# A six-layer decoder kernel: each VectorE filter, convolution and norm instruction waits for its own predecessor instead of for the last one issued

## The reference, cut to what matters

```python
x = _layernorm(x + L0_attn(x));  x = _layernorm(x + L0_xattn(x, ctx));  x = _layernorm(x + L0_ffn(x))   # a, b, c
x = _layernorm(x + L1_attn(x));  x = _layernorm(x + L1_xattn(x, ctx));  x = _layernorm(x + L1_ffn(x))   # d, e, f
```

```python
q = silu(dwconv(hs @ q_proj_w.T, q_conv_w)); k = ...; v = ...   # causal depthwise convolution, 4 taps
delta = delta_rule(q, k, v, beta)                                # chunkwise, with a triangular inverse
short = fir(v, fir_short_w)     # causal depthwise filter, 3 taps
long_ = fir(v, fir_long_w)      # causal depthwise filter, 31 taps
o = wgt0 * short + wgt1 * long_ + wgt2 * delta + wgt3 * v        # weights from a small gate network
```

## Time and profile before

| | |
|---|---|
| median of 3 runs | 4067.72 us (4062.06 to 4068.14) |
| profiled execution, its own time | 4060.48 us |
| its span, first to last instruction | 4058.7 us |
| PE busy | 3306.0 us, 81% |
| DVE busy | 2622.4 us, 65% |
| ACT busy | 1637.3 us, 40% |
| POOL busy | 341.9 us, 8% |
| mean granted TensorE clock | 0.932 of full speed |

### The profile page before, as it was taken

The page is one execution under the profiler, slowest core; times in us unless marked ns, Lnnn a source line. Parts: engine busy times, 40 slices in busy tenths (PEclk is TensorE's granted clock), DMA queues, the critical chain, the costliest instruction groups (busy, mean ns, idle before and its releaser), DMA issues.

```text
span 4058.7 us, 64443 instructions
## 1 busy us (share of the span) xinstructions
PE 3306.0 (81%) x22532; PEld 2516.1 (62%) x22532; DVE 2622.4 (65%) x5927; ACT 1637.3 (40%) x3066; POOL 341.9 (8%) x696
## 2 busy tenths in 40 slices
PE   1678988889797988889798888979798888978664
PEld 0456766767575766667576676757566666756452
DVE  4324667585776767576676758577676757666653
ACT  1423453544435354444435354443535444342311
POOL 1000101010100101010100101010010101010100
PEclk9788999999999999999999999999999999999766
DMA  2011211121111112111121111111111211111000
GB/s 71 21 58 47 64 37 53 35 57 42 45 48 38 53 35 64 35 51 42 38 55 38 53 35 56 42 42 47 43 53 35 60 38 51 42 33 54 9 6 3
DMA packets 185756, 175.65 MB, mean 43 GB/s; under 512 B 59208, under 2 KB 147936, under 8 KB 185440
## 3 DMA queue, kind: packets, MB, share of 16 engines
q1 hardware_dynamic: 185440, 171.27, 14.6%
HBM read 156.55 MB, written 14.68 MB: 42 GB/s over the span
## 4 chain that ended last, share of the span: by engine, by line
PE 38%; issue 26%; DVE 25%; ACT 6%; POOL 2%; DMA 1%; PEld 0%; SPq 0%; PEldq 0%; DVEq 0%; ACTq 0%; POOLq 0%
PE bank L703 13%; DVE region L1796 4%; PE bank L938 4%; PE bank L791 3%; ACT pt_f L1200 3%; DVE nm_f L1577 2%; PE bank L737 2%; PE bank L771 2%; PE bank L1020 1%; PE bank L784 1%; PE bank L1099 1%; PE bank L1031 1%; POOL rn L672 1%; ACT qT_f L1221 1%; PE bank L1040 1%
## 5 line engine op out<-in xcount | busy, mean ns | idle before, releaser
L1200 ACT ACTIVATE pt_f<-bank 128x512 f32<-128x512 f32 x768 | 416.2, 594 | 281.5 <-PE bank L771 280.9
L938 PE MATMUL bank<-c_w,c_hb 128*128 128x256 f32 x2048 | 511.1, 389 | 10.0 <-PEq L1173 6.6
L703 PE MATMUL bank<-xTc,c_w 128*128 128x256 f32 x2048 | 488.9, 388 | 16.4 <-DVE yc L1729 15.7
L1796 DVE SCALAR_TENSOR_TENSOR region<-vpad,cols,region 128x256 f32<-128x256 f32 x1024 | 450.5, 481 | 15.4
L938 PEld LDWEIGHTS bank<-c_w,c_hb 128*128 128x128 f32 x2048 | 378.2, 193 | 98.1 <-issue 26.0
L703 PEld LDWEIGHTS bank<-xTc,c_w 128*128 128x128 f32 x2048 | 383.9, 193 | 79.5 <-DVE yc L1729 21.3
L737 PE MATMUL bank<-identb,split_f 128*102 128x128 bf16 (+1 forms) x4096 | 296.6, 241 | 151.1 <-DVE split_f L1562 109.6
L1299 ACT ACTIVATE c_hb<-bank,cols 128x256 f32<-128x256 f32 x512 | 215.0, 471 | 484.5 <-PE bank L703 484.5
L737 PEld LDWEIGHTS bank<-identb,split_f 128*102 128x102 bf16 (+1 forms) x4096 | 284.2, 144 | 181.7 <-issue 124.8
L1577 DVE TENSOR_REDUCE nm_f<-bank 128x2 f32<-128x512 f32 x512 | 315.9, 685 | 122.5 <-PE bank L758 119.2
L771 PE MATMUL bank<-qT_f,kT_f 102*128 102x256 bf16 (+1 forms) x1536 | 276.1, 282 | 116.0 <-ACT pt_f L1200 91.6
(11 more groups left out here) (310 smaller groups left out, 5442.9 us busy)
## 6 DMA issues: line engine op xcount, KB each, us to landing
c_w<-in_c_w SPq DMA_DIRECT2D x256, 512.0 KB, 3.8
gram_scratch<-region SPq DMA_DIRECT2D x32, 256.0 KB, 2.1
x<-in_x SPq DMA_DIRECT2D x16, 256.0 KB, 4.2
x<-in_ctx SPq DMA_DIRECT2D x16, 256.0 KB, 4.4
ctxb<-in_ctx SPq DMA_DIRECT2D x16, 256.0 KB, 3.6
out_dram<-x SPq DMA_DIRECT2D x16, 256.0 KB, 2.3
region<-gram_scratch SPq DMA_DIRECT2D x128, 8.0 KB
inverse_scratch<-region SPq DMA_DIRECT2D x32, 64.0 KB
```

Source lines behind the costliest of these rows:

```text
L703: mm = pe.matmul(out_ap, l, r, start=(i == 0), stop=(i == len(pairs) - 1))
L938: mm = pe.matmul(PS[use][:, t * D:(t + 1) * D], c_hb[:, k, t * P:(t + 1) * P], c_w2[:, e % W_SLOTS, k, :], start=(k == 0), stop=(k == HC - 1))
L1200: act.activation(dst, PS[use].rearrange("p (c s) -> p c s", c=c), func, **kw).then_inc(*PS.drained(use))
L1796: ins = dve.scalar_tensor_tensor(dst[:, c, :], x, w_[:, c, k:k + 1], dst[:, c, :], ALU.mult, ALU.add)
```

## The change: what it does, and the diff

`mark(g, ins)` raises the counter like `link`, but returns its value and waits for nothing. The filters keep, for each of the two tiles, the value of the instruction that last wrote it (`summed[c]`), and an instruction waits for that one. The convolution does the same with six (`tapped[j]`). In `ln_stats` each `bn_aggr` waits for the `bn_stats` of its own half; the `link` behind the pair of `bn_aggr` stays. The operations, their order, their shapes and the segments stay; no `link` stands at the end of a filter segment any more. Every filter instruction but the last now raises the counter.

```diff
+            def mark(g, ins):
+                chain[g] += 1
+                ins.then_inc(s_chain[g], 1)
+                return chain[g]
...
             def ln_stats(b, l, g, src):
-                for t in range(T):
-                    ins = dve.bn_stats(stats[g][:, t, :], src[:, t, :])
-                link(g, ins)
-                for t in range(T):
+                made = [mark(g, dve.bn_stats(stats[g][:, t, :], src[:, t, :])) for t in range(T)]
+                for t in range(T):
+                    dve.wait_ge(s_chain[g], made[t])
                     ins = dve.bn_aggr(mv[g][:, t, :], stats[g][:, t, :])
                 link(g, ins)
...
+                tapped = [0] * 6
                 for k in range(3):
                     for j in range(6):
                         if k == 0 and j % 2 == 0:
                             dve.wait_ge(*PS.taken(f"d_{'qkv'[j // 2]}", b))
+                        if k:
+                            dve.wait_ge(s_chain["d"], tapped[j])
                         ins = dve.scalar_tensor_tensor(cv[:, j, :], pre[:, j, k:k + S], w[:, j, k:k + 1], cv[:, j, :], ALU.mult, ALU.add)
-                    link("d", ins) if k < 2 else ins.then_inc(*d_cv.up)
+                        if k < 2:
+                            tapped[j] = mark("d", ins)
+                ins.then_inc(*d_cv.up)
...
+                summed = [0] * C
                 def fir(dst, w_, K, k):
                     for c in range(C):
                         x = vpad[:, c, KL - K + k:KL - K + k + S]
                         if k == 0:
                             ins = dve.tensor_scalar(dst[:, c, :], x, w_[:, c, 0:1], None, ALU.mult)
                         else:
+                            dve.wait_ge(s_chain["d"], summed[c])
                             ins = dve.scalar_tensor_tensor(dst[:, c, :], x, w_[:, c, k:k + 1], dst[:, c, :], ALU.mult, ALU.add)
-                    return ins
+                        if (K, k, c) == (KL, KL - 1, C - 1):
+                            ins.then_inc(*d_fir.up)
+                        else:
+                            summed[c] = mark("d", ins)
...
                     for k in range(i * len(taps) // n, (i + 1) * len(taps) // n):
-                        ins = fir(*taps[k])
-                        if k == len(taps) - 1:
-                            ins.then_inc(*d_fir.up)
-                        else:
-                            link("d", ins)
+                        fir(*taps[k])
```

## The result

The changed kernel takes 4027.26 us in the median of 7 runs (4006.67 to 4040.98), against 4067.72 of the kernel before (4062.06 to 4076.79, 7 runs). The ratio is 0.9901, with a 95% interval of 0.9887 to 0.9915: 40 us less, 35 to 46 by the interval. The gain is 1% of the kernel. I had forecast 28.4 us less, 4039. The profiled execution took 4022.17 us, its span is 4020.5.

What follows compares the result with a forecast made beforehand. Neither TensorE (81% busy) nor VectorE (65%) alone was the bound; segment order makes them wait in turn. Terms of 20.7 + 3.4 + 2.9 + 0.9 + 0.5 = 28.4 us gave 4039, with 8 in 10 from 4012 to 4066.

Steps and rivals of the forecast that it cites:

- The cost of a link: VectorE filters: waiting for the instruction directly before costs 0.126 us, 0.086 of lost overlap and 0.04 of gap.
- rival 2: No overlap is won: the engine empties anyway, or link and new waits cost alike; 4067, no change; chance 0.04.
- fir1: Filter segment before an expert's sum: hands over 0.78 us earlier per pass, all gained because TensorE waits 1.12 there.
- fir5 and the norm of a: Filter segment and norm before TensorE's 0.62 wait for x: 0.45 and 0.08, together 0.53 us a pass.
- fir0, fir2 and fir3, fir4 and fir6, the convolution: VectorE segments before waits for other engines: fir0 leaves 0.04 us a pass, the others save VectorE time worth nothing.
- Rival 3: All that VectorE saves shows in the time: 80 us, 3988; chance 0.08.
- A norm: First bn_aggr no longer waits for the second bn_stats: 0.08 us taken, at least 0, at most 0.12.
- Outside the loop: Iterations other than the thirteen loop passes: n = 16, n = 17, n = 2 and norms elsewhere give 7.7 us.
- The loop: Thirteen passes, each 1.59 us shorter, give 20.7 us.
- Rival 1: TensorE meets another wait before the pass ends, so only the other iterations' 7.7 us stay: 4060; chance 0.12.
- the sum: VectorE's savings counted only where TensorE waits: 1.59 us a pass, 28.4 us in all.
- the slack segments: Filter segments fir2, fir3, fir4 and fir6, behind which VectorE waits for TensorE: their savings were taken as worth nothing.

Runs made afterwards that it cites:

- every_link: The changed kernel, but each filter instruction waits for the one directly before it; 4072.75 us against 4070.28, ratio 1.0008.
- norms_only: The kernel before with only the norms' waits changed, filters and convolution as before; 4057.17 us against 4067.84, ratio 0.9981.
- fir1_only: The kernel before with new waits only in the ten instructions of filter segment fir1; 4046.64 us against 4070.28, ratio 0.9956.
- two parts: New waits in fir1 alone on the kernel before, ratio 0.9956; the changed kernel with old waits in fir1 alone, ratio 0.9991.
- filters_only: The kernel before with only the filters' waits changed, convolution and norms as before; 4035.82 us against 4070.28, ratio 0.9921.
- two pairs with TensorE's work changed: Kernel before and changed kernel, both with 128-column small products, or both with resized fillers in TensorE's idle time; medians 27.8 and 28.3 us apart.
- the third pair: Kernel before and changed kernel, both with the first, oversized fillers on TensorE; 4163.26 and 4103.41 us, ratios 1.0226 and 1.0096.
- before_wide: The kernel before with the last doubling's 32 small TensorE products computing 128 columns instead of 64; 4072.62 us against 4067.84, ratio 1.0012.
- before_filled: The kernel before with unread products, resized to 0.44 us each, filling TensorE's idle time; 4070.12 us against 4068.10, ratio 1.0005.
- after_wide: The changed kernel with the last doubling's small TensorE products computing 128 columns instead of 64; 4044.80 us against 4067.84, ratio 0.9952.

## Why the prediction was right, and where its size was off

The step, the place and the sign held, and most terms of the pass are met to a tenth of a microsecond:

- The cost of a link, 0.126: ten instructions 4.04 and twenty 8.00, forecast 4.04 and 7.99; every_link measured 5.17 for ten, with the 0.521 taken from the same row. The wait for the second-last instruction and the signal on each cost nothing. With that rival 2 is out: a step is 0.395 with no wait for the neighbour and 0.521 with one. The Trainium skill, "VectorE: DVE Perf Modes", "The DRAIN you can't avoid", says that the next instruction starts only when the pipe is empty, with or without semaphores in the chain. The measurement speaks against it, and decides.
- fir1, 0.78: 0.77 in VectorE, 0.8 in TensorE's lead.
- fir5 and the norm of a, 0.53: 0.46.
- fir0, fir2 and fir3, fir4 and fir6, the convolution: nothing. TensorE's lead doesn't change behind fir0 to fir4 but at fir1, and VectorE's idle time grew behind fir4 (5.79 to 6.86) and the convolution. Behind fir6 it shrank (1.84 to 0.84), since the product waited for came at full clock. Rival 3 is out by that.
- A norm, 0.08: VectorE's `tensor_scalar` comes 1.00 behind the start of bn_stats instead of 1.07, so 0.07.
- Outside the loop, 7.7: 7.6. That this is met so closely is luck. By the starts of L672 the iterations ahead of the loop gave 0.6, where 0.9 and most of the norms' 0.5 were forecast, n = 16 gave 3.0 of 3.4, and n = 17 and 18 gave 4.0, where 2.9 and a little for norms were forecast.
- The loop, 20.7: 30.7. This is the term that was off. I took TensorE's work between the waits as fixed in length, so that a pass is shorter by exactly what its waits give up. It isn't fixed: its clock is at half speed for some stretches of a pass, and which instructions fall into them hangs on when these come. Before the change one of these stretches lay on products that nothing hid (3.49 against 1.99 us); after it, in most passes, not. The waits aren't fixed either: a drop ahead of one can swallow it. Rival 1, the gain in the loop given back, is out for the whole change by the 228.7, but it is what norms_only does from its second pass on.

What the experiments show of the cause: a small edit of VectorE's waits moves the clock's drops (norms_only, fir1_only, every_link), and the loop's time follows them and not the edit (18 + 4 us in two parts against 40 together; a net cost of 15 to 22 us seen as 3). Where the drops are like those of the kernel before and leave the waits alone, in the first passes of norms_only and filters_only, a pass is shorter by what the sum says (0.23 and 1.46, forecast 0.24 and 1.35). Where a drop covers fir1's wait it isn't: the later passes of the same two kernels last the same. In two pairs with TensorE's work changed, 27.8 and 28.3 us separate the medians (24 and 29 by the ratios), near 28.4. That those agree to a microsecond with the sum is luck: the third pair stands at 60, and by the intervals of the ratios each distance is uncertain by some 8 to 11 us, my estimate.

What stays open: why a drop comes at one place and not at another. Taking away one drop (before_wide) or the idle time ahead of two (before_filled) brought others. So for one aligned pass I can show that what exceeds the sum, 1.9 us, lies in stretches where the clock differs; for the 10 us of the whole loop it is what the passes suggest, and no run shows that this amount would come again with another edit.

The range, 4012 to 4066, held the median with room on both sides; its lower end was set by the wrong reason, the slack segments. The forecast's own range, 4026 to 4052, held it by 1 us.

## What to carry to other kernels

Where one engine walks through independent sums, let each instruction wait for its own predecessor: on VectorE a wait for the instruction directly in front costs 0.126 us of overlap and gap here, a wait for the one before that nothing. Count the gain only at places where another engine waits, from the timeline. In a loop whose TensorE drops in clock more than once a pass, treat such a sum as good to a third at best: compare passes with like drops, look whether the wait that you count on is still there in them, and don't judge an edit worth 0.3% of a kernel by its median alone, since a cost can hide and a gain can double.

## What the runs showed of the hardware that I had not expected

- The loop takes few lengths. With quite different waits most passes lasted 231.9 to 232.3 (the kernel before, norms_only, every_link, filters_only, after_wide), or 228.7 to 229.2, or alternated between 229.2 and 231.7. Twelve of the 13 passes of the kernel before lie within 0.15 us of one another, the last is shorter for its seam. A saving of 0.24 a pass was absorbed from the second pass of norms_only on, one of 0.8 gave 18 us.
- TensorE's clock fell with the engine busy: at 2113.7 behind 3.5 us of products of 64 rows by 64 columns. The same products stand in the same place of the changed kernel, where it didn't fall in the first ten passes. The Trainium skill, "TensorE: Matmul & The Clock Gate", Part 1, says that the clock is either at half or at full rate, by recent activity, and that the monitor doesn't start with the kernel, so that the same kernel changes speed at other instructions from run to run. The two levels, 3.49 against 1.99 us for the same products, agree, and so do the passes of one kernel that differ only in their drops.
- A product of two float32 operands with 256 columns is recorded as two instructions and took 0.44 us (24 records of fillers in 5.35 us in before_filled).
